# Conditional adapter on one core: batch 0's down-projection weights and biases in one transfer of 4 KB rows in place of two of 2 KB rows

## What is computed

```
Wd, bd, Wu, bu, g, b = W_down[stream], b_down[stream], W_up[stream], b_up[stream], ln_w[stream], ln_b[stream]
h = einsum('bsh,bhk->bsk', x, Wd) + bd        # 512 x 512 by 512 x 256
h = gelu(h, approximate=False)
h = einsum('bsk,bkh->bsh', h, Wu) + bu        # 512 x 256 by 256 x 512
h = x + h
out = (h - mean) * rsqrt(var + 1e-5) * g + b
```

## Time and profile before

| what | value |
|---|---|
| median of the timed runs | 65.13 us (65.05, 65.13, 65.72) |
| profiled execution, its own time | 64.73 us |
| its span, first to last instruction | 63.0 us |
| around the span | 1.73 us |
| PE, DVE, POOL, ACT busy | 86%, 75%, 71%, 54% |
| mean granted TensorE clock | 0.971 of 2.4 GHz |

### The profile page before, as it was taken

How to read it: one execution, slowest core, us unless ns; L and a number is a source line. 1 busy time by engine, 2 the same in 40 slices (tenths; PEclk the granted TensorE clock), 3 DMA queues, 4 the chain that set the end, 5 groups by cost and what they waited for, 6 DMA issues and landing times.

```text
span 63.0 us, 916 instructions
## 1 busy us (share of the span) xinstructions
PE 54.2 (86%) x254; PEld 43.4 (69%) x254; DVE 47.5 (75%) x106; ACT 34.1 (54%) x54; POOL 44.8 (71%) x53
## 2 busy tenths in 40 slices
PE   0999699999999999999999999999999999970000
PEld 0979344887888788878888888788998899640000
DVE  0039998976799487979997397999969898898400
ACT  0070122989994059999700999960369954403000
POOL 4600061088989999999999999999995399464600
PEclk9999999999999999999999999999999999999855
DMA  0797999998999999999999999891008002553090
GB/s 0 234 416 223 335 317 387 374 411 328 382 413 419 415 416 421 400 434 401 413 411 403 416 447 413 361 372 55 16 5 333 0 0 96 237 204 129 0 338 0
DMA packets 5058, 17.92 MB, mean 284 GB/s; under 512 B 694, under 2 KB 694, under 8 KB 4668
## 3 DMA queue, kind: packets, MB, share of 16 engines
q1 hardware_dynamic: 4608, 16.80, 67.8%
q10 hardware_dynamic: 444, 1.06, 4.7%
HBM read 13.66 MB, written 4.19 MB: 283 GB/s over the span
## 4 chain that ended last, share of the span: by engine, by line
PE 73%; DMA 5%; SPq 4%; issue 3%; DVE 3%; POOL 3%; ACT 1%; POOLq 1%
PE y_ps L686 11%; PE y_ps L719 10%; PE y_ps L693 10%; PE hid_ps L647 7%; PE hid_ps L639 7%; PE hid_ps L643 7%; PE hid_ps L604 6%; DMA w_raw<-weights 5%; PE y_ps L702 5%; SPq L185 4%; PE hid_ps L667 3%; PE hid_ps L663 3%; PE hid_ps L659 3%; POOL result L294 2%; DVE result L508 1%
## 5 line engine op out<-in xcount | busy, mean ns | idle before, releaser
L273 POOL TENSOR_TENSOR x_lo<-x_raw,x_hi 128x512 fp32r<-128x512 f32 x10 | 13.0, 1317 | 0.4 <-ACT x_hi L356 0.3
L284 POOL TENSOR_TENSOR wu_lo<-w_raw,wu_hi 128x512 fp32r<-128x512 f32 x8 | 10.5, 1318 | 3.1 <-ACT wu_hi L366 3.1
L686 PE MATMUL y_ps<-wu_hi,hid_hi 128*128 128x512 f32 x32 | 12.5, 395 | 0.0
L693 PE MATMUL y_ps<-wu_lo,hid_hi 128*128 128x512 f32 x32 | 12.2, 391 | 0.0
L719 PE MATMUL y_ps<-wu_hi,hid_lo 128*128 128x512 f32 x32 | 12.0, 397 | 0.0
L498 DVE SCALAR_TENSOR_TENSOR y_ps<-y_ps,mean_var,ln_gb 128x512 f32<-128x512 f32 x16 | 11.5, 752 | 0.0
L481 DVE BATCH_NORM_STATS2 stats<-y_ps 128x6 f32<-128x512 f32 x16 | 10.5, 689 | 0.7 <-PE y_ps L693 0.5
L508 DVE SCALAR_TENSOR_TENSOR result<-y_ps,rstd,ln_gb 128x512 f32<-128x512 f32 x12 | 8.7, 745 | 1.6 <-POOL rstd L289 1.4
L639 PE MATMUL hid_ps<-x_hi,wd_hi 128*128 128x512 f32 x20 | 8.2, 410 | 0.0
L279 POOL TENSOR_TENSOR wd_lo<-w_raw,wd_hi 128x512 fp32r<-128x512 f32 x6 | 7.8, 1306 | 0.4 <-ACT wd_hi L360 0.4
L378 ACT ACTIVATE hid_hi<-hid_ps,w_raw 128x512 fp32r<-128x512 f32 x6 | 4.1, 684 | 6.8 <-PE hid_ps L647 6.8
(11 more groups left out here) (51 smaller groups left out, 94.9 us busy)
## 6 DMA issues: line engine op xcount, KB each, us to landing
x_raw<-x_cols SPq DMA_DIRECT2D x6, 512.0 KB, 9.3
x_raw<-x_rows SPq DMA_DIRECT2D x3, 1024.0 KB, 11.3
out<-result SPq DMA_DIRECT2D x6, 512.0 KB, 6.6
w_raw<-weights SPq DMA_DIRECT2D x4, 512.0 KB, 9.6
ln_gb<-ln_rows SPq DMA_DIRECT2D x4, 512.0 KB, 14.0
w_raw<-weights SPq DMA_DIRECT2D x3, 516.0 KB, 11.9
x_raw<-x_cols ACTq DMA_DIRECT2D x2, 512.0 KB, 3.8
out<-result SPq DMA_DIRECT2D x4, 256.0 KB, 2.4
```

Source lines behind the costliest of these rows:

```text
L273: nc.gpsimd.tensor_tensor(x_lo[:, b % 2, k, :], x_raw[:, b, k, :], x_hi[:, b % 2, k, :].bitcast(F32), ALU.subtract).then_inc(x_lo_done, 1)
L284: nc.gpsimd.tensor_tensor(wu_lo[:, b % 2, j, :], raw_wu(b, j, j + 1)[:, 0, :], wu_hi[:, b % 2, j, :].bitcast(F32), ALU.subtract).then_inc( ...
L686: nc.tensor.matmul(y_ps[:, t, :], hid_hi[:, p, j, t * P:(t + 1) * P], wu_hi[:, p, j, :], start=False, stop=False, skip_group_check=True)
L693: product = nc.tensor.matmul(y_ps[:, t, :], hid_hi[:, p, j, t * P:(t + 1) * P], wu_lo[:, p, j, :], start=False, stop=last, skip_group_chec ...
```

## The change

Batch 0's Wd and its biases are loaded by `load_wd(0)`, the same function that loads the other batches': one transfer of 128 rows of 4128 bytes (516 KB) in place of one of 128 rows of 2048 bytes (256 KB) and one of 128 rows of 2080 bytes (260 KB). One semaphore, `wd_in[0]`, stands for both, and both waits of `down_whole` and the wait of ACT are for it.

```diff
-        first_wd_in = [sem(f"first_wd_in{c}") for c in range(2)]
-        wd_in = [first_wd_in[1]] + [sem(f"wd_in{b}") for b in range(1, B)]
+        wd_in = [sem(f"wd_in{b}") for b in range(B)]
...
-            sp.dma_start(w_raw[:, 0, 0:HALF * BN], row_of(0)[:, 0:HALF * BN]).then_inc(first_wd_in[0], DMA)
-            sp.dma_start(w_raw[:, 0, HALF * BN:WD_END], row_of(0)[:, HALF * BN:WD_END]).then_inc(first_wd_in[1], DMA)
+            load_wd(0)
             load_x(1, 0)
             load_wu(0)
             load_x(1, 1)
...
-            for c in range(2):
-                act.wait_ge(first_wd_in[c], DMA)
+            act.wait_ge(wd_in[0], DMA)
             nc.scalar.activation(wd_hi[:, 0, :, P:BN], raw_wd(0, 0, KT)[:, :, P:BN],
...
                     if k % HALF == 0:
                         pe.wait_ge(x_in[0][k // HALF], DMA)
-                        pe.wait_ge(first_wd_in[k // HALF], DMA)
+                        pe.wait_ge(wd_in[0], DMA)
```

## The result

The changed kernel took 66.57 us (median of 6 executions, 65.72 to 66.67), the kernel before 65.22 us in the same comparison (64.94 to 65.72). The ratio is **1.0194, 95% interval 1.0147 to 1.0241**: slower, and by more than twice the 0.55 us that was forecast. The six times are 65.72, 65.90, 66.50, 66.64, 66.66 and 66.67 us, 0.95 us from lowest to highest against 0.78 of the kernel before, and four of the six lie at 66.5 or above. Measured once more beside other kernels, it gave 1.0144 (1.0066 to 1.0222).

What follows compares the result with a forecast made beforehand. PE was taken to bound the kernel, hanging rigidly on its first product's start, set by Wd's first half landing. +0.60 for the later start and -0.05 given back make +0.55 us: 65.68 us on the 65.13 median, range 65.0 to 66.2.

Steps and rivals of the forecast that it cites:

- Part 1: PE's first product waits for all 516 KB of Wd, landing at 7.5 instead of 6.90, and starts at 7.63: +0.60 us.
- Part 2: PE's later work and SP's later loads shift with the late start; ACT's slack gives a little back: -0.05 us.
- Part 3: Edits costed at nothing: ACT's rounding stays at 7.61, PE's second wait is met, following loads issue 0.58 us earlier.
- Rival B: Wd lands later than its bytes explain, after 7.65, delaying PE's start by up to 1.6 us more: 66.0 to 67.2; chance 0.12.
- Rival A: Single transfer of Wd lands no later, at 6.9 to 7.2, costing 0.0 to 0.3 us: 65.1 to 65.4; chance 0.20.
- Rival C: TensorE's clock falls while PE idles from 6.54 to 7.63, slowing its first products: 66 to 69 us; chance 0.04.

Runs made afterwards that it cites:

- the experts first: Kernel before, with SP reading experts 1 to 3 right behind Wd's two halves and only then issuing batch 0's Wu and batch 1's x; ratio 1.0612.
- the quarter without a gap: Kernel before, with Wd's first quarter as first transfer, awaited by k = 0, and the rest with biases as second, awaited by k = 1; ratio 0.9987.
- two halves and a gap: Kernel before, with SP reading expert 0's index once more between Wd's second half and batch 1's x; ratio 0.9932, again 0.9932.
- both halves awaited: Kernel before, its two transfers of Wd kept, with PE's first product waiting for both; ratio 1.0122, median 66.01 us.
- rows of 4096 bytes: Changed kernel, its single transfer cut to exactly 4096 bytes per row, with the biases coming with batch 0's Wu; ratio 1.0153.
- the gap: Changed kernel, with SP reading expert 0's index once more behind Wd, so batch 1's x is issued at 6.63 us; ratio 1.0063.
- three of 4 KB: Changed kernel, with three added 4 KB transfers right behind Wd, then an extra index read before batch 1's x; ratio 1.0047.

## Why the prediction was wrong

**What held.** The start of PE's first product carries the kernel, rigidly. Over 18 profiled executions (all kernels but the one with the experts first, and the quarter without a gap, which has a second wait for Wd inside its first products), the execution's own time less the start of the first product is always between 57.5 and 58.2 us, while the start itself goes from 7.03 to 8.78:

| execution | own time | first product | difference |
|---|---|---|---|
| before | 64.73 | 7.03 | 57.70 |
| before, second profile | 65.08 | 7.28 | 57.80 |
| two halves and a gap | 64.63 | 7.08 | 57.55 |
| both halves awaited | 65.54 | 7.75 | 57.79 |
| changed | 65.90 | 7.98 | 57.92 |
| changed, third profile | 66.19 | 8.19 | 58.00 |
| rows of 4096 bytes | 66.71 | 8.78 | 57.93 |

So Part 1's path and Part 2's claim that a late start reaches the end hold. Of the 0.05 us that Part 2 gave back nothing is seen: the difference is 57.90 to 58.00 in the changed kernel and 57.70 and 57.80 in the kernel before, larger rather than smaller, and over all kernels it scatters by 0.7. It is a small term, and no run isolates it.

**What failed.** It is the landing in Part 1: "I take 7.5 ... the range around it is 7.4 to 7.65". The second half's landing was the right row for the bytes, and with a gap behind it the single transfer does land at 7.6, near 7.5. But that sum took the single transfer as undisturbed by what follows, and Part 3 put the earlier issue of the following loads at nothing, with the words that they "can't slow Wd either, if the queue serves them in its order". They do slow it. The clean price of waiting for all bytes is 0.7 us (1.0044 against 0.9932, and 7.78 against 7.08), near the forecast's 0.60. The loads behind add to it: the changed kernel is at 1.0144 to 1.0194 where the gap gives 1.0063, which is (0.0144 - 0.0063) x 65.2 = 0.5 to 0.9 us. The gap also helps the kernel before, by 0.0068 x 65.2 = 0.4 us, though its profiles do not show through what. The parts come to 0.7 + (0.5 to 0.9) - 0.4 = 0.8 to 1.2 us, and the ratios 1.0144 and 1.0194 are 0.9 and 1.3 us.

By the constant difference the median of the first measurement, 66.57, stands, as an estimate, for a first product at about 66.57 - 57.9 = 8.7 and a landing near 8.5. The second one, 65.97, stands for a first product at 8.1. By how much the first product is late thus differs from one measurement to the other, and why is open.

**The rivals.** Rival B, with a chance of 0.12, is what happened, in its nearer part: Wd later than its bytes explain. The row that pointed to it was on the table: 5.8 us for the next 512 KB, 1.6 us more than its place in the queue explained. I named it as an upper end, had no cause for it that I could price, and so gave it little weight. With a gap the same transfer landed in 3.4 us. Whether it had been late by the same effect as Wd is not certain: with the gap it still had big loads close behind it, and only the ones close ahead were gone. The rival's own mechanism, that what held the third transfer falls on an earlier one, is therefore not shown. Rival A was wrong: no single transfer of Wd landed before 7.56. Rival C did not occur at the place in question; the granted clock in the windows stayed 1.00 while PE idled from 6.5 to 8.0, and the products of L600 took the same 3.67 us. Part 3's other edits cost nothing, as forecast; its claim that ACT would start at 7.61 as now was tied to the landing and moved with it, to 7.87.

**The base.** The profile of before was of a fast execution (7.03); a typical one starts, as an estimate, at about 65.13 - 57.8 = 7.3, and in the one other profile (7.28) this is because of the transposes. I noted the 0.40 us between profile and median and did not ask what it was. It was the same place, the start of the first product, but not the landing of Wd.

The Trainium skill, DMA: Bandwidth & Descriptors, section "Rules for kernel authors", advises to coalesce small transfers into one large transfer and puts the best bandwidth at 1 MiB or more per transfer. At 516 KB the rule's gain is not there (with the gap, two halves with both awaited and a single transfer measure alike, 1.0044 and 1.0063), and its price is: the first consumer waits for the last byte. The same page, section "Queues, rings and completion order", says that a later descriptor may finish before an earlier one. That fits with bytes of later loads passing before Wd was complete, but no run here shows by which step of the hardware they delay it, and that stays open.

## What to carry to other kernels

When a transfer gates the first real work of the engine that bounds the kernel, split it so that the first product waits for as few bytes as it needs, and keep big loads that nobody needs yet out of the queue until it is through: here 2 to 3 us of distance were worth 0.7% to the better kernel and 0.8 to 1.3% to the worse. Try it on the transfer in question, since not every transfer with big loads behind it was late here. Merging two transfers does not only add the second one's bytes to the wait, it also moves everything behind it closer. If one row of the profile is later than its bytes explain, as the third transfer was here, find out why before taking its neighbour as undisturbed; and before holding a load back, look for whoever stands in line behind its consumer (the experts first cost 6%).

## What the runs showed of the hardware

- Big loads queued 0.45 us behind Wd delay it (ratios 1.0144 and 1.0194, against 1.0063 with 3 us between them), three of 4 KB do not (1.0047). The delay differs from one execution to the next: the same 516 KB landed in 4.05, 4.25 and 4.48 us in three profiles of one kernel. A transfer of 512 KB issued 2 us or more behind the big one ahead of it took 3.1 to 3.4 us, with other big loads as close as 0.5 us behind it.
- The sixteen transposes ahead of the first product took from 2.33 to 3.67 us, in executions of kernels that don't differ there, while the granted clock in these windows is 1.00 throughout. They run at two paces: most took 0.27 us in the profile of the kernel before, and most took 0.42 us where PE waits for both halves, which is what the warm-up products ahead of them take in both. No row tells what makes the pace change earlier in one execution than in another.
- When batch 1's x came late, DVE's rounding of a 128 x 512 tile took 1.44 and 1.52 us in place of 0.42 in the kernel before, and its subtraction 1.64 in place of 0.69, while POOL ran L284 (2.70 us from 12.78) and L273 (1.27 us from 15.93) beside it. The Trainium skill, SBUF — State Buffer, section "SBUF: two separate sides", states that some DVE operations and GpSimd hold a common pair of ports in turn; the rows fit, but no run took the two apart.
